# Five PSUM banks divided anew between attention scores and row maxima, and PSUM-emptying work moved from VectorE to ScalarE

## The reference, cut to what matters

```python
def _L0_attn_ref(x, Wq, bq, Wk, bk, Wv, bv, Wo, bo):
    q = proj(Wq, bq); k = proj(Wk, bk); v = proj(Wv, bv)
    q = _apply_rope(q, cos, sin) * scale
    k = _apply_rope(k, cos, sin)
    attn = jnp.einsum('bhsd,bhtd->bhst', q, k)
    attn = jax.nn.softmax(attn, axis=-1)
    out = jnp.einsum('bhst,bhtd->bhsd', attn, v)
    return jnp.einsum('bsd,ed->bse', out, Wo) + bo
def _L0_ffn_ref(x, W1, b1, W2, b2):
    Wq1 = _quantize(W1)          # values -1, 0, 1
    Wq2 = _quantize(W2)
    h = jax.nn.relu(jnp.einsum('bsd,fd->bsf', x, Wq1) + b1)
    return jnp.einsum('bsf,df->bsd', h, Wq2) + b2
x = _layernorm(x + _L0_attn_ref(x, ...), axis=-1)
x = _layernorm(x + _L0_ffn_ref(x, ...), axis=-1)
```

## Time and profile before

| | us |
|---|---|
| median of 3 runs (3389.06 to 3391.72) | 3390.58 |
| the profiled execution | 3384.53 |
| its span in the trace | 3382.7 |
| PE busy (weight loads PEld) | 3261.7 (1784.6) |
| DVE busy | 2985.4 |
| ACT busy | 2512.8 |
| POOL busy | 2168.1 |

### The profile page before, as it was taken

The page is one execution under the profiler, slowest core; times in us unless marked ns, Lnnn a source line. Parts: engine busy times, 40 slices in busy tenths (PEclk is TensorE's granted clock), DMA queues, the critical chain, the costliest instruction groups (busy, mean ns, idle before and its releaser), DMA issues.

```text
span 3382.7 us, 81458 instructions
## 1 busy us (share of the span) xinstructions
PE 3261.7 (96%) x30726; PEld 1784.6 (53%) x30726; DVE 2985.4 (88%) x5670; ACT 2512.8 (74%) x4884; POOL 2168.1 (64%) x2479
## 2 busy tenths in 40 slices
PE   6999999999999999999999999999999999999975
PEld 4434555555555555555555555555555555544444
DVE  7888999999999999999999999999999999999921
ACT  2777777777777777777777777777777777777740
POOL 3535766766776676676677667667766766734456
PEclk7999999999999999999999999999999999999987
DMA  6444454355345445534444543553454454344110
GB/s 186 103 94 98 98 114 104 92 116 116 96 100 117 99 97 114 113 92 110 114 98 101 114 105 91 115 118 92 104 116 100 97 113 108 91 89 82 35 43 26
DMA packets 310792, 339.09 MB, mean 100 GB/s; under 512 B 77056, under 2 KB 259200, under 8 KB 310400
## 3 DMA queue, kind: packets, MB, share of 16 engines
q1 hardware_dynamic: 310400, 333.89, 43.2%
HBM read 193.27 MB, written 140.51 MB: 99 GB/s over the span
## 4 chain that ended last, share of the span: by engine, by line
PE 94%; POOL 2%; DVE 1%; ACT 1%; DMA 1%; issue 1%; SPq 0%; POOLq 0%; DVEq 0%; ACTq 0%
PE ob L716 30%; PE sc L699 29%; PE job L571 25%; PE ms L688 9%; ACT prob L821 1%; POOL hid_r L1188 1%; DVE mxp L1069 1%; PE ms L571 0%; PE job L624 0%; PE ob L571 0%; POOL ka L1280 0%; PE sc L571 0%; DVE hid L1000 0%; DVE w_sb L1105 0%; POOL hid_r L1186 0%
## 5 line engine op out<-in xcount | busy, mean ns | idle before, releaser
L952 DVE TENSOR_REDUCE mxp<-ms 128x1 f32<-128x512 f32 x4064 | 2620.9, 682 | 246.1 <-PE ms L688 200.0
L821 ACT ACTIVATE prob<-sc 128x512 f32<-128x512 f32 x4096 | 2224.8, 597 | 687.1 <-PE sc L699 662.5
L699 PE MATMUL sc<-qa,ka 50*128 50x512 f32 x4096 | 1545.4, 443 | 27.5 <-ACT prob L821 27.5
L688 PE MATMUL ms<-ka,qa 48*128 48x512 f32 x4064 | 1539.5, 445 | 0.4 <-DVE mxp L952 0.4
L699 PEld LDWEIGHTS sc<-qa,ka 50*128 50x128 f32 x4096 | 683.2, 184 | 1119.0 <-ACT prob L821 970.5
L716 PE MATMUL ob<-prob,v_sb 128*17 128x512 f32 x8192 | 1078.2, 598 | 0.3
L688 PEld LDWEIGHTS ms<-ka,qa 48*128 48x128 f32 x4064 | 679.1, 184 | 6.6 <-DVE mxp L952 4.2
L1167 POOL TENSOR_TENSOR ve<-mv,eps_sb 128x2 f32<-128x2 f32 x128 | 25.2, 197 | 517.3 <-DVE mv L979 517.3
L1188 POOL TENSOR_TENSOR hid_r<-hid,hid_r 128x512 fp32r<-128x512 f32 x256 | 328.7, 1284 | 20.5
L571 PEld LDWEIGHTS job<-h_t,w_sb 64*128 64x128 f32 x3840 | 259.7, 185 | 23.3
L716 PEld LDWEIGHTS ob<-prob,v_sb 128*17 128x17 f32 x8192 | 136.0, 95 | 256.1 <-issue 255.2
(11 more groups left out here) (135 smaller groups left out, 2817.6 us busy)
## 6 DMA issues: line engine op xcount, KB each, us to landing
qk_parts<-parts SPq DMA_DIRECT2D x124, 512.0 KB, 4.3
ka<-qk_parts SPq DMA_DIRECT2D x378, 128.0 KB, 4.6
qa<-qk_parts SPq DMA_DIRECT2D x378, 128.0 KB, 7.3
attention<-at_st SPq DMA_DIRECT2D x128, 256.0 KB, 3.0
v_ones<-v_st SPq DMA_DIRECT2D x64, 272.0 KB, 2.4
v_sb<-v_ones SPq DMA_DIRECT2D x64, 272.0 KB, 8.6
xn<-x SPq DMA_DIRECT2D x64, 256.0 KB, 4.8
ao<-attention SPq DMA_DIRECT2D x128, 128.0 KB
```

The lines of the kernel that those rows point to most:

```text
L688: nc.tensor.matmul(ms[upto(b, g, NS1, at) % MS_BANKS][:, :], operand(qa, b, g, j, ROWS)[:, qt * P:(qt + 1) * P], operand(ka, b, g, j, ROWS ...
L699: nc.tensor.matmul(sc[upto(b, g, HG * STEPS, n) % SC_BANKS][:, :], operand(ka, b, g, j, ROWS + MROWS)[:, tt * P:(tt + 1) * P], operand(qa, ...
L821: nc.scalar.activation(prob[st_ % 2][:, j, :], sc[upto(b, g, HG * STEPS, n) % SC_BANKS][:, :], ACT.Exp).then_inc(s["exp_done"], 1)
L952: nc.vector.reduce_max(mxp[(b * G + g) % 2][:, kh, j * TT + qt:j * TT + qt + 1], ms[upto(b, g, NS1, at) % MS_BANKS][:, :], AX.X).then_inc( ...
```

## The change

`SC_BANKS` goes from 2 to 3 and `MS_BANKS` from 3 to 2; the total stays five. ScalarE takes over the second job bank of the projections, which VectorE took (`take_key_half` is gone), and one of the two odd FFN tiles of each job pair (`take_odd_hidden`), so that VectorE keeps one of four. ScalarE's `finish_rest` moves ahead of exponential 3. Two entries of VectorE's tables move by a part.

```diff
-SC_BANKS = 2
-MS_BANKS = 3
+SC_BANKS = 3
+MS_BANKS = 2
-FIRST_NORM = {(1, 1): "sum 0", (1, 2): "sum 1", (2, 2): "stats 0", (4, 0): "stats 1", (4, 2): "moments 0"}
-SECOND_SUMS = {(15, 1): "sum 0", (15, 2): "sum 1"}
+FIRST_NORM = {(1, 1): "sum 0", (1, 3): "sum 1", (2, 2): "stats 0", (4, 0): "stats 1", (4, 2): "moments 0"}
+SECOND_SUMS = {(15, 1): "sum 0", (15, 3): "sum 1"}
@@ banks_of
-                return ((sc[0], sc[1]), (ms[2], ms[1]))[int(name[1]) % 2]
+                return ((sc[0], sc[1]), (sc[2], ms[1]))[int(name[1]) % 2]
@@ scalar
+            def take_odd_hidden(b, g, n, tile):
+
+                act.wait_ge(s["f_odd_taken"], upto(b, g, FT // 2, n))
+                nc.scalar.activation(hid[n % 2][:, 1, :], tile, ACT.Relu, bias=b1_sb[:, 2 * n + 1:2 * n + 2]
+                                     ).then_inc(s["f_odd_taken"], 1)
+
@@ finish_rest
                     take_hidden(*at, int(name[1]), job[0][:, TQ:2 * TQ])
+                    take_odd_hidden(*at, int(name[1]), job[1][:, TQ:2 * TQ])
+                elif stage == "proj":
+                    proj_job(*at, name, (1,))
@@ batch of scalar
                         exps(b, g, st_, 2)
-                        exps(b, g, st_, 3)
                         for job_ in jobs_at(b, g, st_, tail):
                             finish_rest(job_)
+                        exps(b, g, st_, 3)
@@ vector: take_key_half is removed; its batch
-                                if stage == "proj" and part == 1:
-                                    take_key_half(*at, name)
-                                elif name in ("f1", "f3") and part in (1, 2):
-                                    p = part - 1
-                                    take_hidden(*at, int(name[1]) - 1 + p, job[1][:, p * TQ:(p + 1) * TQ])
+                                if name in ("f1", "f3") and part == 1:
+                                    take_hidden(*at, int(name[1]) - 1, job[1][:, 0:TQ])
```

More of the change, by code:

```diff
@@ L979, in moments_of @@
                     nc.vector.bn_aggr(moments[:, tl, :], stats[:, tl, :]).then_inc(s["moments" + tag], 1)
[L981 to L994, removed]
             def take_hidden(b, g, n, tile):
```

## The result

The changed kernel takes 3659.96 us (median of 4 runs, 3658.05 to 3660.64) against 3390.38 us of the kernel before on the same chip: a ratio of 1.0794, 95% interval 1.0776 to 1.0813. It is slower by 270 us. The forecast was 3647 us, in a range of 3605 to 3700.

A forecast was written before the change was run, and what follows sets the result against it. Before, a loop through two exponentials sets the step; after, one through two reductions: 16 x 3.32 + 0.6 = 53.7 us a unit against 49.60, 258 us over 63 units, edges -2, median +6: 3647 us, range 3605 to 3700.

The forecast's parts named there:

- The loop and its place: Every ordinary step: fourth maximum waits for the second reduction, starts at 1.91 us, making the step 3.32 us; 92%.
- One sign: Trace after: TensorE's waits would be put down to VectorE's `mxp`, and hardly any to ScalarE's `prob`.
- The release of 0.06 us and the lone maximum's 0.42 to the weighing: Unit 0, step 1, before: maximum starts 0.06 us after the second reduction ends, weighing 0.42 after that maximum.
- the choice of 0.43 for the FFN steps: Eight FFN steps: weighing 0.43 us behind the fourth maximum; 0.36 instead would take 35 us off.
- The extras of steps 2, 4 and 12: VectorE's other work between the first two reductions: 0.42 us in step 4, 0.1 each in 2 and 12; 0.6 a unit.
- The edges: Last unit +1 and -3 us, sequence 0 -2, the twelve maxima before the first step +2: together -2 us.
- The 6 us by which the median was to lie above the profiled execution: Added to the profiled execution's 3641 us to give the forecast median of 3647 us.
- The moved work at nothing: Up to 2.4 us a unit leaving VectorE, 2.4 joining ScalarE, and the table moves: all counted as nothing.
- the cover that the prediction named: Steps after f1, f3: late ScalarE queue needed only by third score and weighing; uncovered, 13 us per 0.1 us late.
- The third score bank: Fourth score needs the first exponential, not the second: steps 0 to 5 and 7 take 2.85 us if nothing else stops TensorE.
- The one on the other side: Rival: reductions free the banks in time, 47.7 us a unit, 3271 us; gain and loss meet at 1.69 us; 4%.
- The clock: Granted clock stays at 1.00; rival: it falls to 1.2 GHz for a tenth of the time, 3900 us, 2%.

The follow-up runs named there:

- The two places of the added reciprocal: Changed kernel plus an unused 128x32 VectorE reciprocal every step: between first and second reduction 3851.06 us, behind the second 3660.27 us.
- the two cuts of the columns: Changed kernel with the step's reductions over fewer of the 512 columns: 256 columns 3297.23 us, 384 columns 3395.81 us.
- the banks alone: Kernel before with three score and two maxima banks, last tail's spare pair renamed, no work moved: 3663.27 us.
- the two runs with the old banks: Changed kernel with two score and three maxima banks: 3469.99 us; the same with both `finish_rest` emptyings behind the fourth exponential: 3465.73 us.

## Why the prediction was right

- **The loop and its place** were right. The fourth maximum waits for the second reduction in every ordinary step, with 1.90 to 1.92 + 0.43 + 0.99 us where 1.91 + 0.43 + 0.98 stood. The two places of the added reciprocal and the two cuts of the columns show it by intervention, not only by the rows. One sign came out otherwise: waits put down to `prob` are still many on the weight loads of the scores, but not where they hold anything up.
- **The release of 0.06 us and the lone maximum's 0.42 to the weighing**, taken from the one step of the kernel before where five maxima met three banks, held in the whole kernel. So did the choice of 0.43 for the FFN steps, where a stream would give 0.36; the 35 us kept for it in the range were not needed.
- **The extras of steps 2, 4 and 12** were the term that was mis-sized. I took 0.6 us a unit, 0.42 for step 4 and 0.1 each for the other two; they measure 3.46, 3.81 and 3.49 against 3.32, which is 0.80. The unit grew by 4.32 us instead of 4.1, which is 14 us over 63 units. In step 4 the first reduction starts 0.63 us after the first score (1719.01 - 1718.38) and not at 0.56; in the kernel before it was 0.64 (1586.69 in the earlier trace rows, with the first score at 1586.05), and I took the spacing alone.
- **The edges** were put at -2 us and came out at +4. By first scores, the part ahead of the first step grew by 2.3 us, units 0 to 3 by 16.5 (four steady units by 17.3), units 60 to 62 by 16.1 (three steady units by 13.0), and what follows the first score of unit 63 shrank by 1.0. The excess of units 60 to 62 goes with the clock, below.
- **The closeness of the median** is in part luck. From execution to execution the profiled time grew by 276 us against the 256 of the sum, 20 short: 14 for the units and 6 for the edges. The 6 us by which the median was to lie above the profiled execution did not come back (3659.96 against 3660.64) and hid a third of that.
- **The moved work at nothing** was right for the changed kernel (3660 against 3663 with the banks alone), and so was the cover that the prediction named: the fourth exponential is needed by the next step's third score. That cover is the third score bank, as the two runs with shorter reductions show, and the two runs with the old banks take it away: 75 to 80 us. The 13 us that the prediction put down to a lack of cover stand for a lateness of 0.1 us; steps 10 and 12 came out 0.52 and 0.59 longer, and the tables' move added 0.21 in step 0.
- **The third score bank** is worth most of what was worked out once the maxima hold nothing up: the run with 256 columns gives 3297 us, 93 less than before, where the rival's sum said 3271, 120 less. In a unit (48.37 against 47.7) the difference is mostly steps 0, 1 and 4.
- **The rivals.** The one on the other side (relieved VectorE, faster) fell: its point was a release at 1.69 us, and the release stayed at 1.90. The kernel before doesn't follow VectorE's work even when a third of it is gone. On the Trainium skill's rule (Perfetto Trace Analysis, Identifying the Most-Contended Engine) the runs say that the engine with the highest occupancy after TensorE, at 88%, was not the one to relieve; its advice in the same page not to judge TensorE by busy time agrees with the 96% on both pages.
- **The clock** stayed up in the steady units, as forecast, but not quite everywhere. The windows of a steady unit and of the last unit (first and third line) show 1.00. From unit 58 on no projections are left, and in each of the units 59 to 62 the clock stood at its lower level for a stretch of 3.4 us (second line); in unit 62 TensorE had waited 0.43, 0.23 and 0.34 us for `mxp` in the ten microseconds before. These four took 54.65 us each, unit 58 without such a stretch 53.09, and units 60 to 62 of the run with the banks alone, also without it, 53.4. My estimate from these lengths is 1.6 us a unit, 6 us of the 276; without the three in units 60 to 62 the edges would come to about -1.

```profile
1704.98:1758.89 53.91, 53.38 (x486) 29.69 (x482) 44.80 (x85) 40.60 (x81) 34.30 (x39) 1.00 0.43 98
...
3344.70:3348.10 3.40, 3.40 (x20) 0.65 (x12) 1.76 (x3) 1.48 (x3) 1.35 (x2) 0.50 0.00 0
...
3486.00:3534.00 48.00, 45.80 (x372) 21.16 (x368) 16.14 (x39) 37.60 (x74) 20.08 (x27) 1.00 0.11 36
```

No run here beats the kernel before with the full computation. The one run that is clearly faster leaves out half of the maxima's columns. A sixth bank, three for each kind, would be the full-work counterpart of that run; it was not tried, as all eight banks are in use.

## What to carry to other kernels

When banks are shared out between two producers in one in-order queue, look for the last release inside a period and not for the busier engine: a bank given to the quicker emptier (0.50 us apart) was taken from the slower one (0.60), and nearly all of the 0.23 us that a step gained (3.32 against 3.09) is that difference, counted twice. What stands between the two emptyings that end such a loop costs most of its time (0.21 us of a row of 0.34); what stood behind them was free here. Work moved to an engine with a quarter of its time to spare can still be late in the one step where it is bunched, and a change of two parts can hide that, as the third score bank did here: run each part alone.

## What the runs showed of the hardware that was not expected

- TensorE's granted clock stayed at its lower level longer at the start of the changed kernel. The windows of the changed kernel around the first steps, and of the kernel before:

```profile
91.00:97.70 6.70, 6.52 (x32) 3.47 (x32) 3.39 (x6) 2.87 (x7) 2.01 (x2) 0.50 0.17 29
```

```profile
91.00:100.00 9.00, 9.00 (x78) 4.76 (x79) 7.80 (x14) 5.79 (x12) 2.44 (x2) 0.95 0.00 1
```

  It is 0.50 (1.2 GHz) up to 97.70 us in the one and 0.95 on average from 91 us in the other. With two maxima banks the five maxima of each early step came with waits of 0.18 to 0.32 us for `mxp` before the clock rose. Why it rose later was not tested; unit 0 as a whole took 58.9 us instead of 52.9, 6 us more where 4 were due.
- The reduction behind the added reciprocal had a row of 0.63 us instead of 0.69, so that an inserted instruction of 0.34 us moved the end of the next one by 0.21. Behind the small reduction of 0.17 us in step 4 the row was 0.68; what makes the difference was not tested.
